# A three-stage decoder kernel: the last bodies of its software pipeline written out by hand for each engine

## The chip, the cores and the metric

The kernel runs on one core of a Trainium2 chip. The metric is device time of one execution in microseconds, the median of several; lower is better. Five engines with instruction streams of their own take part: TensorE (PE, matmuls into the eight banks of PSUM), ScalarE (ACT), VectorE (DVE), GpSimd (POOL) and SyncE (SP, which here issues all DMAs of the steady part). They meet only at semaphores that the kernel counts by hand.

## What is computed

`x` is (16, 256, 512) float32, `ctx` has the same shape.

```
x = layernorm(x + attention(x))           # 16 heads of 32, q/k/v/o with low-rank updates
x = layernorm(x + x * scan(ctx*ctx))      # r = decay*r + ctx^2 along the sequence
h = gelu(silu(bitlinear(x, w1, b1)))      # 512 -> 2048; rms norm, 8-bit rounding of rows, ternary weights
h = layernorm(h) * ln_g + ln_b            # over 2048
x = layernorm(x + bitlinear(h, w2, b2))   # 2048 -> 512
```

## The kernel before, in words

The work is cut into 16 batches of 256 rows, each batch into two tiles (q = 0, 1) of 128 rows. A batch goes through a software pipeline of four steps: body `j` does the attention of batch j, the two first layernorms and the first linear layer (`f`, eight blocks of 512 columns) of batch j-1, the wide layernorm and rounding of batch j-2, and the second linear layer (`y`, 16 matmuls for each tile) and the last layernorm of batch j-3. Each engine has its own `body(j)` with the order of its instructions written out by hand; `alive(j, lag)` leaves out the steps whose batch does not exist. `batches` (L187) runs the body for j = 0 to 18, so that the last three bodies, 16, 17 and 18, only empty the pipeline, in the order that was laid out for a full one.

What the change and the prediction touch:

- TensorE: `qk`, `scores`, `shifted`, `weighted` are attention, in banks 0 to 5. `o` (L1176, L1180, matmuls at L1081), `r` (L1183, matmuls at L1187), `f` (L1190, L1195) and `y` (L1199, L1202) share banks 6 and 7: `take` (L1150) finds the last user of the bank and waits for the instruction that read it. `y` reads `hqT`, of which there is one.
- SyncE: `transpose_z` (L302) moves the rounded tile of h, transposed, into `hqT` by two DMA transposes (L307), after `y` of the tile before it has read `hqT`. `transpose_x` (L294, L299) does the same for the input of `f`. `store_out` (L290) writes a tile of the result.
- ScalarE: `silu` (L615, L621), `gelu` (L624, L627), `h_var` (L630, L637, a square with a sum), `h_norm` (L640, L642), `z_square` (L645, L652), `zq_store` (L609, L612, the rounded tile as bf16, which `transpose_z` reads), `normalise` (L593, L597), `xq_store` (L600, L606).
- VectorE: `layernorm1_sum`, `layernorm2_sum`, `layernorm3_sum` (L846, L854, L940: a sum, then its statistics at L842 and L844), `quantise_x` (L862, from L881 to L901), `z_add` (L904, L907), `z_max` (L909, L912), `quantise_z` (L915: five steps on one column, then the rounding at L937).
- GpSimd: `g_mul` (L476, L479, h times `g_tile`), `neg_mean`, `h_rstd` (L463), `z_rms`, `inverse_std1` to `3` (small steps on one or two columns), `res1`, `res2` (L429, L436), which add bias rows.

The chain of a tile after `gelu` is: `h_var`, `h_rstd`, `h_norm`, `g_mul`, `z_add`, `z_max` and `z_square`, `z_rms`, `quantise_z`, `zq_store`, `transpose_z`, `y`, `layernorm3_sum`, `inverse_std3`, `normalise(3)`, `store_out`. Each engine executes in its own order, so a step that waits holds what stands behind it.

Of the kernel before, what the change touches and what calls it, by code (L numbers as in the profile page):

```python
# [7 lines left out]
F32 = mybir.dt.float32  # L8
# [36 lines left out]
NROWS = 3  # L45
LAST_LAG = 3


def decoder_kernel(nc, x, xT, ctxT, W, L, bq, bk, bv, bo, decay, w1T, b1, ln_g, ln_b, w2T, b2, out):
    b1_scratch = nc.dram_tensor("b1_scratch", (NPART, INNER), BF16, kind="Internal").ap()  # L50

    with ExitStack() as ctx:
# [57 lines left out]
        junk = sb("junk", [P, INNER], BF16)  # L110
        fz = sb("fz", [P, NT, 12], F32)
        fs = sb("fs", [P, NT, 8], F32)

# [32 lines left out]
        u_mul = sem("u_mul")  # L146
        u_tern = sem("u_tern")


# [37 lines left out]
        def batches(body):  # L187

            for j in range(NB + LAST_LAG):
                body(j)  # L190
# [17 lines left out]

        def bank_of(name, index):
            return bank[bank_no[name, index]]  # L210

# [24 lines left out]
        def _(sp):  # L236
# [73 lines left out]
            def body(j):  # L310
                if alive(j, -1):
                    load_xT(j + 1)
                if alive(j, 3):
                    transpose_z(j - 3, 1)
                if alive(j, 3):
                    store_out(j - 3, 0)
                if j == 0:
                    load_ctx(0)
                    load_rows(0)
                    sp.wait_ge(u_b1, 5)  # L320
                    for k in range(NPART):
                        sp.dma_start(b1_scratch[k].rearrange("(p f) -> p f", p=P),
                                     b1_parts[:, k, :]).then_inc(u_b1_out, 16)
                    sp.wait_ge(u_b1_out, 16 * NPART)
                    sp.wait_ge(u_zero, 1)
                    for k in range(NPART):
                        sp.dma_start(b1_rows[k * NPART:(k + 1) * NPART, :], b1_scratch).then_inc(u_b1_in, 16)
                    for n in range(4, 8):
                        ffn_chunk(n)
                else:  # L330
                    if alive(j, 0):
                        load_ctx(j)
                    if alive(j, 3):
                        store_out(j - 3, 1)
                    if alive(j, 1):
                        transpose_x(j - 1)
                    if alive(j, 2):
                        transpose_z(j - 2, 0)
                    if alive(j, 0):
                        load_rows(j)  # L340
            batches(body)
            wait(sp, "out_stored", NB - 1, 32)

# [4 lines left out]
        def _(po):  # L348
# [68 lines left out]
            def inverse_std3(b, q):  # L417

                r = rstd[:, 2, :, q:q + 1]
                wait(po, "ln3", b, 3 * (q + 1))  # L420
                po.tensor_scalar(r[:, R_VE, :], mean_var[:, 2, q, 1:2], 1.0, EPS, ALU.mult,
                                 ALU.add).then_inc(S["rstd3"], 1)
# [53 lines left out]
            def g_mul(b, q):  # L476

                wait(po, "h_normed", b, q + 1)
                po.tensor_tensor(h_of(b, q)[:, :], h_of(b, q)[:, :], g_tile[:, :], ALU.mult).then_inc(S["g_mul"], 1)  # L479

            def z_rms(b, q):
# [6 lines left out]
                wait(po, "z_rms", b, 2 * q + 1)  # L488
                po.tensor_tensor(fz[:, q, Z_RMS:Z_RMS + 1], f[:, H_ZMS:H_ZMS + 1], neg_half[:, 0:1],
                                 ALU.pow).then_inc(S["z_rms"], 1)  # L490
# [11 lines left out]
            def body(j):  # L502
# [35 lines left out]
                if alive(j, 0):  # L538
                    attn_split(j, 3)

            batches(body)


# [3 lines left out]
        def _(ac):  # L547
# [35 lines left out]
            def v_store(b, q):  # L583
                wait(ac, "pv_ready", b - 2, 4)
                wait(ac, "v_ready", b, q + 1)
                ac.activation(v_sb[b % 2][:, q, :], bank_of("v", q), ACT.Identity).then_inc(S["v_stored"], 1)

# [27 lines left out]
            def silu(b, q):  # L615
                for n in range(NF):
                    u = NF * q + n
                    wait(ac, "f_ready", b, u + 1)
                    if n == 0:
                        wait(ac, "hqT_loaded", b - 2, 32 * (q + 1))  # L620
                    ac.activation(h_of(b, q)[:, n * FW:(n + 1) * FW], bank_of("f", u), ACT.Silu,  # L621
                                  scale=qx[:, X_DEQ, q:q + 1]).then_inc(S["silu_done"], 1)
# [63 lines left out]
            def body(j):  # L686
# [76 lines left out]
                if alive(j, 1):  # L763
                    silu(j - 1, 1)
                    gelu(j - 1, 0)
                    gelu(j - 1, 1)

            batches(body)


# [3 lines left out]
        def _(dv):  # L774
# [71 lines left out]
            def layernorm1_sum(b, q):  # L846

                wait(dv, "o_ready", b, q + 1)
                wait(dv, "res1", b, q + 1)
                dv.tensor_tensor(rows_of(b)[:, q, :], bank_of("o", q), rows_of(b)[:, q, :],  # L850
                                 ALU.add).then_inc(S["ln1"], 1)
                statistics(1, b, q, 3 * q + 1, rows_of(b)[:, q, :])

            def layernorm2_sum(b, q):  # L854

                wait(dv, "rT_ready", b, q + 1)
                wait(dv, "norm1", b, q + 1)
                dv.scalar_tensor_tensor(rows_of(b)[:, q, :], bank_of("r", q), SCAN_SCALE, rows_of(b)[:, q, :],  # L858
                                        ALU.add, ALU.mult).then_inc(S["ln2"], 1)
# [44 lines left out]
            def z_add(b, q):  # L904

                wait(dv, "g_mul", b, q + 1)
                dv.tensor_tensor(h_of(b, q)[:, :], h_of(b, q)[:, :], b_tile[:, :], ALU.add).then_inc(S["z_added"], 1)  # L907

            def z_max(b, q):  # L909

                wait(dv, "z_added", b, 2 * q + 1)
                dv.tensor_reduce(fz[:, q, Z_MAX:Z_MAX + 1], h_of(b, q)[:, :], axis=AX_X, op=ALU.max,  # L912
                                 apply_absolute_value=True).then_inc(S["z_added"], 1)

            def quantise_z(b, q):  # L915

                def f(k):
                    return fz[:, q, k:k + 1]

                step = [6 * q]  # L920

                def done(ins):
# [10 lines left out]
                done(dv.tensor_tensor(f(Z_MUL), f(Z_SC), f(Z_RMS), ALU.mult))  # L933
                wait(dv, "ln3", b - 1, 3 * q + 1)
                done(dv.tensor_scalar(f(Z_DEQ), f(Z_INV), w_mean[:, 1:2], None, ALU.mult))
                wait(dv, "z_squared", b, q + 1)
                dv.tensor_scalar(h_of(b, q)[:, :], h_of(b, q)[:, :], f(Z_MUL), ROUND, ALU.mult,  # L937
                                 ALU.add).then_inc(S["z_quant"], 1)

            def layernorm3_sum(b, q):  # L940

                wait(dv, "y_ready", b, q + 1)
                wait(dv, "res2", b, q + 1)
                dv.scalar_tensor_tensor(rows_of(b)[:, q, :], bank_of("y", q), fz[:, q, Z_DEQ:Z_DEQ + 1],
                                        rows_of(b)[:, q, :], ALU.mult, ALU.add).then_inc(S["ln3"], 1)
# [52 lines left out]
            def body(j):  # L998
# [52 lines left out]
                if alive(j, 0):  # L1051
                    scan(j)

            batches(body)


# [3 lines left out]
        def _(pe):  # L1060
# [119 lines left out]
            def o_second_half(j, q):  # L1180
                split_product(bank_of("o", q)[:, :], o_terms(q, (2, 3)), first=False).then_inc(S["o_ready"], 1)

            def r(j, q):  # L1183

                p = take(j, "r", q, "scan_done", j - 1, 5)
                for kc in range(KC):
# [3 lines left out]
            def f(j, u):  # L1190

                q, n = divmod(u, NF)
                p = take(j, "f", u, "xqT_loaded", j - 1, 16)
                for kc in range(KC):
# [157 lines left out]
```

## Time and profile before

| | us |
|---|---|
| median of 3 runs | 1128.77 (1127.43 to 1133.42) |
| the profiled execution, its own time | 1124.67 |
| its span, first to last instruction | 1122.9 |
| busy in the span: PE, DVE, ACT, POOL | 952.4, 887.3, 828.3, 601.0 |
| mean granted clock of TensorE | 0.945 of full speed |

The span is 1.8 us shorter than the profiled execution's time, which is 4.1 us under the median. Times in the rows below are counted from the start of the span. A busy time adds up the instructions of an engine. The record of an instruction also holds the time for which it stood in the engine without being able to run. A timeline row that says x16 is sixteen like instructions in a row, with the time from the first one's start to the last one's end; brackets give the idle time before it and what ended that. The last instruction of body 15 on each engine ends between 998 and 1011 us; what comes after it is bodies 16 to 18.

### The profile page before, as it was taken

The page shows a single profiled execution, that of the slowest core. Times are in us where ns is not written, and L with a number is a line of the kernel's source. Part 1 is how long each engine was busy: PE and PEld are TensorE (multiplying, and loading weights), DVE is VectorE, ACT ScalarE, POOL GpSimd, SP SyncE. Part 2 cuts the span into 40 slices and gives each one's busy share as a digit, 9 for nine tenths or more (in the row PEclk, how much of TensorE's full clock was granted, in tenths as well). Part 3 has the DMA queues.
Part 4 walks back from the last instruction along what each step waited for, and adds up shares of the span by engine and source line. Part 5 has one row for each costly group of instructions (what it writes and reads, how often), then busy time and mean ns, then how long its engine had stood idle before and what let it go on. Part 6 is the DMA issues. An engine that isn't in the chain of part 4 may idle for free.

```text
span 1122.9 us, 23509 instructions
## 1 busy us (share of the span) xinstructions
PE 952.4 (85%) x9388; PEld 653.1 (58%) x9388; DVE 887.3 (79%) x1470; ACT 828.3 (74%) x955; POOL 601.0 (54%) x769
## 2 busy tenths in 40 slices
PE   4878878998989898999999898989899998873424
PEld 2666656675757666665757575766667575531201
DVE  5378858888897979798988989797979898885442
ACT  3456677887879787878788787978787878775651
POOL 3213428384756657482938475565738293747250
PEclk8989898999999999999999999999999999977756
DMA  8512100213131212213221313122221222121112
GB/s 309 208 71 101 43 27 20 69 49 78 49 78 20 75 52 51 62 53 69 48 79 49 78 48 78 20 70 57 50 58 57 69 48 60 49 59 28 40 28 66
DMA packets 106350, 73.67 MB, mean 66 GB/s; under 512 B 91385, under 2 KB 91385, under 8 KB 104450
## 3 DMA queue, kind: packets, MB, share of 16 engines
q1 hardware_dynamic: 105522, 70.34, 23.4%
q8 instruction: 75, 1.23, 0.5%
q10 hardware_dynamic: 720, 1.84, 0.5%
q14 instruction: 33, 0.27, 0.1%
HBM read 41.73 MB, written 8.40 MB: 45 GB/s over the span
## 4 chain that ended last, share of the span: by engine, by line
PE 49%; DVE 31%; ACT 7%; issue 6%; DMA 4%; POOL 2%; SPq 1%; POOLq 0%; ACTq 0%; DVEq 0%
PE bank L1081 17%; PE bank L1202 10%; PE bank L1195 9%; DVE neg_max L793 3%; PE wave L1128 3%; DVE fz L912 3%; DVE h L907 3%; DVE stats L842 3%; PE bank L1140 2%; PE wave L1104 2%; DMA xqT<-xq 2%; PE bank L1144 2%; PE bank L1196 2%; DVE xq L898 2%; DVE rows L858 2%
## 5 line engine op out<-in xcount | busy, mean ns | idle before, releaser
L793 DVE TENSOR_REDUCE neg_max<-wave 128x8 f32<-128x2048 f32 x64 | 146.2, 2285 | 56.8 <-PE wave L1104 56.8
L1195 PE MATMUL bank<-w,xqT 128*128 128x512 fp8e4 x512 | 133.9, 385 | 44.9 <-DMA xqT<-xq 36.9
L479 POOL TENSOR_TENSOR h<-h,g_tile 128x2048 f32<-128x2048 f32 x32 | 148.4, 4638 | 40.4 <-ACT h L642 40.4
L1202 PE MATMUL bank<-w,hqT 128*128 128x512 fp8e4 x512 | 124.7, 400 | 43.3 <-DMA hqT<-h 43.3
L559 ACT ACTIVATE probs<-wave 128x1024 f32<-128x1024 f32 x128 | 124.0, 1021 | 30.9 <-PE wave L1128 30.8
L621 ACT ACTIVATE h<-bank,qx 128x512 f32<-128x512 f32 x128 | 87.0, 687 | 44.6 <-PE bank L1196 44.3
L597 ACT ACTIVATE rows<-rows,rstd 128x512 f32<-128x512 f32 x96 | 74.4, 807 | 55.7 <-POOL rstd L394 19.7
L1202 PEld LDWEIGHTS bank<-w,hqT 128*128 128x128 bf16 x512 | 49.7, 102 | 112.2 <-issue 62.0
L1195 PEld LDWEIGHTS bank<-w,xqT 128*128 128x128 bf16 x512 | 48.5, 99 | 110.6 <-issue 47.1
L378 POOL TENSOR_SCALAR attn_hi<-attn 128x256 fp32r<-128x256 f32 x64 | 26.2, 409 | 157.5 <-DVE attn L826 148.7
L907 DVE TENSOR_TENSOR h<-h,b_tile 128x2048 f32<-128x2048 f32 x32 | 75.5, 2359 | 36.5 <-POOL h L479 36.5
L612 ACT ACTIVATE h<-h,neg_round 128x2048 bf16<-128x2048 f32 x32 | 63.9, 1997 | 32.8 <-DVE h L937 32.8
L1081 PE MATMUL bank<-xT_hi,wq_hi 128*128 128x256 f32 x256 | 78.4, 306 | 8.7 <-DVE wk_lo L787 7.7
L1104 PE MATMUL wave<-qk_parts 32*128 32x256 f32 x1536 | 62.9, 293 | 21.4 <-ACT probs L559 21.3
L433 POOL TENSOR_TENSOR rows<-rows,bo_tile 128x512 f32<-128x512 f32 x32 | 54.7, 1728 | 48.6 <-DMA rows<-x 48.6
L1128 PE MATMUL wave<-qk_parts 32*128 32x256 f32 x1536 | 73.3, 302 | 8.6 <-ACT shift_rows L581 8.6
L652 ACT ACTIVATE junk<-h 128x2048 bf16<-128x2048 f32 x32 | 61.1, 1909 | 24.9 <-DVE h L907 24.8
L381 POOL TENSOR_TENSOR attn_lo<-attn,attn_hi 128x256 fp32r<-128x256 f32 x64 | 73.7, 1152 | 5.3
L642 ACT ACTIVATE h<-h,fs 128x2048 f32<-128x2048 f32 x32 | 66.9, 2090 | 13.1 <-POOL fs L473 13.1
L1128 PEld LDWEIGHTS wave<-qk_parts 32*128 32x128 f32 x1536 | 56.9, 191 | 30.0 <-ACT shift_rows L581 15.4
L1140 PE MATMUL bank<-probs,v_sb 128*32 128x256 f32 x1024 | 69.7, 390 | 4.4 <-ACT probs L559 4.4
L1081 PE MATMUL bank<-xT_lo,wq_hi 128*128 128x256 f32 x256 | 73.3, 286 | 0.0
(151 smaller groups left out, 2821.3 us busy)
## 6 DMA issues: line engine op xcount, KB each, us to landing
ctx_sb<-ctxT SPq DMA_DIRECT2D x16, 512.0 KB, 3.7
rows<-x SPq DMA_DIRECT2D x16, 512.0 KB, 4.0
out<-rows SPq DMA_DIRECT2D x32, 256.0 KB, 2.0
xT_in<-xT SPq DMA_DIRECT2D x15, 512.0 KB, 4.7
h<-w1T SPq DMA_DIRECT2D x4, 1024.0 KB, 5.4
h<-w2T SPq DMA_DIRECT2D x4, 1024.0 KB, 5.6
h<-Wq SPq DMA_DIRECT2D x1, 1024.0 KB, 5.8
h<-Wk SPq DMA_DIRECT2D x1, 1024.0 KB, 9.6
```

Source lines behind the costliest of these rows:

```text
L479: po.tensor_tensor(h_of(b, q)[:, :], h_of(b, q)[:, :], g_tile[:, :], ALU.mult).then_inc(S["g_mul"], 1)
L559: ac.activation(probs[:, kt, :, :], wave[:, :, kt * T:(kt + 1) * T], ACT.Exp, scale=SM_SCALE).then_inc(S["probs_ready"], 1)
L597: ac.activation(rows_of(b)[:, q, :], rows_of(b)[:, q, :], ACT.Identity, scale=r[:, R_USED, :], bias=r[:, R_NB, :]).then_inc(S[f"norm{ln}"], 1)
L621: ac.activation(h_of(b, q)[:, n * FW:(n + 1) * FW], bank_of("f", u), ACT.Silu, scale=qx[:, X_DEQ, q:q + 1]).then_inc(S["silu_done"], 1)
L793: dv.tensor_reduce(neg_max[:, :, :], wave[:, :, :].rearrange("p j (t k) -> p j t k", t=NT), axis=AX_X, op=ALU.max, negate=True).then_inc(S ...
L907: dv.tensor_tensor(h_of(b, q)[:, :], h_of(b, q)[:, :], b_tile[:, :], ALU.add).then_inc(S["z_added"], 1)
L1081: last = pe.matmul(psum, lhsT, rhs, start=(first and i == 0), stop=(final and i == len(pairs) - 1))
L1104: last = pe.matmul(bank[head][:, qt * T:(qt + 1) * T], parts[at, qp, qt * P:(qt + 1) * P], parts[at, kp, :], start=(i == 0), stop=(i == 2))
L1128: last = pe.matmul(bank[head][:, kt * T:(kt + 1) * T], keys, queries, start=(i == 0), stop=(i == 3))
L1140: pe.matmul(bank[4][i * HD:(i + 1) * HD, 0:T], v_sb[b % 2][:, kt, ch:ch + HD], probs[:, kt, i, :], start=(kt == 0), stop=(kt == NT - 1))
L1195: pe.matmul(p[:, :], xqT[:, q, kc, :], w1[:, kc, n * FW:(n + 1) * FW], start=(kc == 0), stop=False)
L1202: last = pe.matmul(p[:, :], hqT[:, k, :], w2[:, k, :], start=(k == 0), stop=(k == FC - 1))
```

## The change

`batches` stops after body 15, and each engine gets a `drain()` of its own that names what is left: the rest of batch 13 (`THIRD`), 14 (`PRIOR`) and 15 (`LAST`). The order in the drains puts the steps of batch 15 ahead of like steps of batch 14 where both are ready.

- Banks: in the drain `o`, `r`, `f` and `y` use all eight (`drain_bank`), each with a wait of its own for the last reader.
- Buffers: the tiles of batch 14 and 15 are transposed into `hqT`, the two halves of `probs` and a `v_sb`, so each `y` has its own. `y` of the three later tiles waits for each half (8 matmuls) by itself.
- `g_mul` of tile 0 of batches 14 and 15 goes from GpSimd to VectorE (`gain`); tile 1 stays.
- In batch 15 the rounding at L937 and the store at L612 are cut into two halves of 1024 columns each.
- `z_square` of batch 14 stands between the two `silu` of batch 15; both `zq_store` of batch 14 stand after `h_norm` of batch 15.
- `fz_last` gives batch 15 its own column values, and some waits are added that go with it.

```diff
+        drain_bank = {("o", LAST, 0): 7, ("o", LAST, 1): 6, ("r", LAST, 0): 2, ("r", LAST, 1): 3,
+                      ("y", THIRD, 0): 0, ("y", THIRD, 1): 1, ("y", PRIOR, 0): 4, ("y", PRIOR, 1): 5,
+                      ("y", LAST, 0): 6, ("y", LAST, 1): 7}
+        drain_bank.update({("f", LAST, u): (4, 5, 6, 7, 0, 1, 2, 3)[u] for u in range(8)})
...
# SyncE
+            def drain_transpose(b, q):
+                for i in range(2):
+                    if b == LAST:
+                        sp.wait_ge(d_zq, 2 * q + i + 1)
+                    else:
+                        wait(sp, "zq_stored", b, q + 1)
...
+                    sp.dma_start_transpose(out=drain_hqT(b, q)[:, 8 * i:8 * (i + 1), :],
+                                           in_=half_rows(b, q)[:, i, :]).then_inc(d_hqT[LAST - b, q, i], 16)
+            def drain():
+                transpose_z(THIRD, 1)
+                transpose_x(LAST)
+                store_out(THIRD, 0)
+                store_out(THIRD, 1)
+                transpose_z(PRIOR, 0)
+                drain_transpose(PRIOR, 1)
+                drain_transpose(LAST, 0)
+                drain_transpose(LAST, 1)
+                store_out(PRIOR, 0)
...
# GpSimd
+            def drain():
+                res1(LAST)
+                neg_mean(PRIOR, 0)
+                neg_mean(PRIOR, 1)
+                inverse_std1(LAST)
+                inverse_std2(LAST)
+                x_rms(LAST)
+                h_rstd(PRIOR, 0)
+                h_rstd(PRIOR, 1)
+                inverse_std3(THIRD, 0)
+                inverse_std3(THIRD, 1)
+                g_mul(PRIOR, 1)
+                res2(LAST)
+                z_rms(PRIOR, 0)
+                z_rms(PRIOR, 1)
+                neg_mean(LAST, 0)
+                neg_mean(LAST, 1)
+                h_rstd(LAST, 0)
+                h_rstd(LAST, 1)
+                g_mul(LAST, 1)
+                z_rms(LAST, 0)
+                z_rms(LAST, 1)
...
# ScalarE
+            def drain_zq_store(q):
+                for i in range(2):
...
+                    ac.activation(half_rows(LAST, q)[:, i, :], h_halves[:, i, :], ACT.Identity,
+                                  bias=neg_round[:, :]).then_inc(d_zq, 1)
+            def drain():
+                zq_store(THIRD, 1)
+                normalise(1, LAST, 0)
+                normalise(1, LAST, 1)
+                h_var(PRIOR, 0)
+                h_var(PRIOR, 1)
+                normalise(2, LAST, 0)
+                normalise(2, LAST, 1)
+                h_norm(PRIOR, 0)
+                xq_store(LAST)
+                h_norm(PRIOR, 1)
+                normalise(3, THIRD, 0)
+                normalise(3, THIRD, 1)
+                silu(LAST, 0)
+                z_square(PRIOR, 0)
+                silu(LAST, 1)
+                z_square(PRIOR, 1)
+                gelu(LAST, 0)
+                gelu(LAST, 1)
+                h_var(LAST, 0)
+                h_var(LAST, 1)
+                h_norm(LAST, 0)
+                h_norm(LAST, 1)
+                zq_store(PRIOR, 0)
+                zq_store(PRIOR, 1)
+                z_square(LAST, 0)
+                z_square(LAST, 1)
+                drain_zq_store(0)
+                drain_zq_store(1)
...
# VectorE
+            def drain():
+                layernorm1_sum(LAST, 0)
+                layernorm1_sum(LAST, 1)
+                layernorm2_sum(LAST, 0)
+                layernorm2_sum(LAST, 1)
+                layernorm3_sum(THIRD, 0)
+                layernorm3_sum(THIRD, 1)
+                quantise_x(LAST)
+                gain(PRIOR, 0)
+                z_add(PRIOR, 0)
+                z_max(PRIOR, 0)
+                z_add(PRIOR, 1)
+                z_max(PRIOR, 1)
+                quantise_z(PRIOR, 0)
+                quantise_z(PRIOR, 1)
+                gain(LAST, 0)
+                z_add(LAST, 0)
+                z_max(LAST, 0)
+                z_add(LAST, 1)
+                quantise_z(LAST, 0)
+                z_max(LAST, 1)
+                quantise_z(LAST, 1)
...
# TensorE
+            def drain():
+                wait(pe, "attn_split", LAST, 8)
+                drain_o(0, "silu_done", PRIOR, 8)
+                drain_o(1, "silu_done", PRIOR, 7)
+                wait(pe, "probs_ready", LAST, 8)
+                wait(pe, "scan_done", LAST, 5)
+                for q in range(NT):
+                    r_product(bank_of("r", q, LAST), q)
+                drain_y(THIRD, 0)
+                drain_y(THIRD, 1)
+                wait(pe, "xqT_loaded", LAST, 16)
+                drain_f(0, "attn_done", LAST, 4)
...
+                drain_f(7, "ln2", LAST, 4)
+                for at, (b, q) in enumerate(((PRIOR, 0), (PRIOR, 1), (LAST, 0), (LAST, 1))):
+                    wait(pe, "silu_done", LAST, at + 1)
+                    drain_y(b, q)
```

After the part shown, GpSimd, ScalarE and VectorE each run the last layernorm of batches 14 and 15, tile by tile, and SyncE stores the four tiles.

## Rows read from the trace of the kernel before

**Rows 1.** windows: busy us of each engine, under full load and at the end
```profile
884.00:1004.00 120.00, 105.56 (x1069) 70.23 (x1068) 103.24 (x175) 94.36 (x109) 70.52 (x93) 0.93 0.22 51
1004.00:1123.00 119.00, 47.74 (x173) 20.96 (x171) 50.36 (x78) 60.74 (x57) 47.08 (x64) 0.69 0.17 38
```

**Rows 2.** timeline of TensorE, end: start us, us, engine, line, [idle before <-releaser]
```profile
1004.79 3.62 PE L1202 MATMUL bank<-w,hqT 128*128 128x512 fp8e4 x16
...
1013.48 0.39 PE L1081 MATMUL bank<-wo_hi,attn_lo 128*128 128x512 f32 x1
1022.73 5.37 PE L1202 MATMUL bank<-w,hqT 128*128 128x512 fp8e4 x16 [8.86 <-DMA hqT<-h]
...
1028.94 0.66 PE L1187 MATMUL bank<-ident,ctx_sb 128*128 128x128 f32 x4 [0.41 <-DVE rows L944]
1050.72 1.86 PE L1195 MATMUL bank<-w,xqT 128*128 128x512 fp8e4 x4 [21.12 <-DMA xqT<-xq]
...
1078.70 6.38 PE L1202 MATMUL bank<-w,hqT 128*128 128x512 fp8e4 x16 [14.31 <-DMA hqT<-h]
...
1110.95 5.63 PE L1202 MATMUL bank<-w,hqT 128*128 128x512 fp8e4 x16 [4.72 <-DMA hqT<-h]
```

**Rows 3.** chain of waits, end: DMA transposes, issue and landing
```profile
1047.18 3.40 DMA xqT<-xq
...
1095.84 1.24 SPq L307
...
1097.12 3.23 DMA hqT<-h
```

**Rows 4.** timeline of ScalarE, end
```profile
1004.99 0.69 ACT L621 ACTIVATE h<-bank,qx 128x512 f32<-128x512 f32 x1 [0.39 <-PE bank L1196]
...
1061.67 1.28 ACT L627 ACT_TABLE_LOAD   x1
...
1066.77 1.99 ACT L637 ACTIVATE junk<-h,fs 128x2048 bf16<-128x2048 f32 x1
...
1080.04 2.09 ACT L642 ACTIVATE h<-h,fs 128x2048 f32<-128x2048 f32 x1 [4.01 <-POOL fs L473]
...
1097.98 2.00 ACT L612 ACTIVATE h<-h,neg_round 128x2048 bf16<-128x2048 f32 x1 [2.16 <-DVE h L937]
...
1119.62 0.81 ACT L597 ACTIVATE rows<-rows,rstd 128x512 f32<-128x512 f32 x1 [9.54 <-POOL rstd L426]
```

**Rows 5.** timeline of VectorE, end
```profile
1041.01 1.22 DVE L881 TENSOR_REDUCE qx<-rows 128x2 f32<-128x1024 f32 x1 [3.75 <-ACT rows L597]
...
1043.86 1.23 DVE L893 TENSOR_SCALAR qx<-qx,w_mean 128x2 f32<-128x2 f32 x1
...
1076.77 2.29 DVE L907 TENSOR_TENSOR h<-h,b_tile 128x2048 f32<-128x2048 f32 x1 [10.65 <-POOL h L479]
...
1093.32 2.28 DVE L912 TENSOR_REDUCE fz<-h 128x1 f32<-128x2048 f32 x1
...
1096.66 1.28 DVE L937 TENSOR_SCALAR h<-h,fz 128x2048 f32<-128x2048 f32 x1
...
1116.62 0.75 DVE L944 SCALAR_TENSOR_TENSOR rows<-bank,fz,rows 128x512 f32<-128x512 f32 x1 [8.65 <-PE bank L1202]
...
1118.13 0.18 DVE L844 BATCH_NORM_AGGREGATE mean_var<-stats 128x2 f32<-128x6 f32 x1
```

**Rows 6.** timeline of GpSimd, end
```profile
1076.82 2.29 POOL L467 TENSOR_SCALAR fs<-fs 128x1 f32<-128x1 f32 x1
...
1082.20 4.52 POOL L479 TENSOR_TENSOR h<-h,g_tile 128x2048 f32<-128x2048 f32 x1 [2.20 <-ACT h L642]
```

**Rows 7.** timeline of GpSimd around 943 us: one addition on GpSimd
```profile
942.89 2.13 POOL L433 TENSOR_TENSOR rows<-rows,bo_tile 128x512 f32<-128x512 f32 x1 [3.01 <-DMA rows<-x]
```

**Rows 8.** timeline of VectorE around 944 us: rounding, then one scan
```profile
942.61 1.29 DVE L937 TENSOR_SCALAR h<-h,fz 128x2048 f32<-128x2048 f32 x1
943.81 1.75 DVE L832 TENSOR_TENSOR_SCAN ctx_sb<-decay_col,ctx_sb 128x256 f32<-128x256 f32 x1
```

More of the change, by code:

```diff
@@ L187, in batches @@
         def batches(body):
-            for j in range(NB + LAST_LAG):
+            for j in range(NB):
                 body(j)
@@ L420, in inverse_std3 @@
                 wait(po, "ln3", b, 3 * (q + 1))
+                if b == LAST:
+                    wait(po, "norm3", PRIOR, q + 1)
                 po.tensor_scalar(r[:, R_VE, :], mean_var[:, 2, q, 1:2], 1.0, EPS, ALU.mult,
@@ L539, in body @@
                     attn_split(j, 3)
+            def drain():
[20 more added lines that the diff above has]
+                z_rms(LAST, 1)
+                for b in (PRIOR, LAST):
+                    for q in range(NT):
+                        inverse_std3(b, q)
             batches(body)
+            drain()
         @block.scalar
@@ L766, in body @@
                     gelu(j - 1, 1)
+            def drain_zq_store(q):
+                h_halves = h_of(LAST, q)[:, :].rearrange("p (i k) -> p i k", i=2)
+                for i in range(2):
+                    if i == 0:
+                        ac.wait_ge(d_round, q + 1)
+                    else:
+                        wait(ac, "z_quant", LAST, 6 * (q + 1))
+                    ac.activation(half_rows(LAST, q)[:, i, :], h_halves[:, i, :], ACT.Identity,
[29 more added lines that the diff above has]
+                drain_zq_store(1)
+                for b in (PRIOR, LAST):
+                    for q in range(NT):
+                        normalise(3, b, q)
             batches(body)
+            drain()
         @block.vector
@@ L1052, in body, with gain @@
                     scan(j)
+            def gain(b, q):
+                wait(dv, "h_normed", b, q + 1)
+                dv.tensor_tensor(h_of(b, q)[:, :], h_of(b, q)[:, :], g_tile[:, :], ALU.mult).then_inc(d_gain_dve, 1)
+            def drain():
[20 more added lines that the diff above has]
+                quantise_z(LAST, 1)
+                for b in (PRIOR, LAST):
+                    for q in range(NT):
+                        layernorm3_sum(b, q)
             batches(body)
+            drain()
         @block.tensor
@@ L1305, in _ @@
             batches(body)
+            drain()
 def kernel(**inputs):
```

105 lines of the change are left out of this document (86 added, 19 removed).

## The prediction

> **What bounds the kernel now.** I read the profile's page first, then stretches. Under full load four engines are busy together: in 120 us TensorE 105.6, VectorE 103.2, ScalarE 94.4, GpSimd 70.5. The last 119 us hold only 47.7, 50.4, 60.7 and 47.1 [rows 1], so there no engine is the bound, but a chain of waits. The change leaves bodies 0 to 15 as they are, so I compare only what follows them.
>
> The timeline of TensorE shows that chain. After `y` of batch 13, tile 0 (1004.79) and the two `o` (last matmul 1013.48), the matmuls come in islands: `y` 13,1 at 1022.73, `f` of batch 15 at 1050.72 after 21.1 us idle, `y` 14,1 at 1078.70 after 14.3, and `y` 15,0 and 15,1, of which the last starts at 1110.95 after 4.7 [rows 2]. The last island waits for the single `hqT`: its transposes start only when the `y` before it has ended.
>
> **The change, part by part.** All times are those of the profiled span; "tile 15,1" is batch 15, tile 1.
>
> *A. From the last `silu` of batch 14 to `f` of batch 15.* That `silu` ends at 1005.7 [rows 4]; `o` waits for it, since both of its banks were read by it. `o` twice takes 5.5 (from the end of `y` at 1008.4 to 1013.9), `r` twice 1.3 (0.66 for one) [rows 2]: 1012.5. `y` 13,0, now behind them, 3.6 at full clock [rows 2]: 1016.2. It used to stand ahead, and `transpose_z` of 13,1 waits for it; the tile itself is stored by 1012.8, since `zq_store` now goes first on ScalarE. A pair of transposes takes 1.28 to the second issue and 3.23 to landing [rows 3], 4.65 with the start of the matmul: 1020.9. `y` 13,1 takes 5.4 to 6.4 after a wait [rows 2]; I take 5.6, the row nearest in idle time: 1026.5. Meanwhile VectorE does both layernorm 1 and 2 sums, and ScalarE both `h_var` of batch 14, all over by 1023, so these cost nothing; without that cover `quantise_x` would wait for them. But `layernorm3_sum` of 13,1 stands ahead of `quantise_x` in VectorE's order: **x of batch 15 waits for `y` of 13**, some 5 us. Sum and statistics 1.7 [rows 5]: 1028.2. `quantise_x` took 6.2, from 1041.01 to the issue of its transpose at 1047.18 [rows 5, 3]; two small steps in it, 1.23 [rows 5] and one like it, stood behind the two additions of `res2`, which now come much later, so 4.4: 1032.6. Transpose 3.4 [rows 3] and the start: 1036.2. It was 1050.7: **14.5 us gained**. Behind the waiting VectorE stand `gain` and `z_add` of batch 14; behind `xq_store` on ScalarE `h_norm` 14,1 (to 1034); neither is needed before 1043.
>
> *B. From `f` to the second `h_norm` of batch 15.* From `f` to the last `silu` it took 10.95 [rows 2, 4]. Two `z_square` of batch 14 now stand in it, nearest row `h_var` with 1.99 each [rows 4]. About 1.6 of these 3.9 is hidden, since with eight banks TensorE runs ahead and the last four `silu` run at 0.69 rather than at the 1.08 of a block. So 13.3: 1049.5. Table load 1.28, two `gelu` 3.8, two `h_var` 4.0, two `h_norm` of 2.09 [rows 4]: 1062.7, where the second ended at 1082.1 before: **19.4 in all**. The 4.9 beyond A, in spite of the `z_square`, come from two things that no longer stand before `h_norm` 15,1: 4.0 of waiting [rows 4] for a GpSimd step that was held 2.29 [rows 6] behind a `g_mul`, and a `zq_store`.
>
> *C. From `h_norm` to the last `y`.* `gain` 15,0 on VectorE, 2.29 as `z_add` is (both read two tiles of SBUF) [rows 5], ends at 1063.0. `g_mul` 15,1 is ready at 1062.8 and takes 4.5 [rows 6]; `z_add` 15,0 is ready at 1063.1. Can they overlap? In the rows an addition on GpSimd ready at 942.89 during a rounding lasted until 945.02, though a scan on VectorE was ready at 943.81; the scan ended at 945.56 [rows 7, 8]. The two took turns, and the one that waited came first. So I take GpSimd first: `g_mul` to 1067.6, `z_add` 15,0 to 1069.9, `z_max` 2.2 to 1072.1, `z_add` 15,1 to 1074.4. Then five small steps 1.06 (from 1095.60 to 1096.66) and two half roundings, 0.65 each [rows 5]: 1076.7; `z_max` 15,1 1079.0; small steps and halves 1081.4. ScalarE is then only busy with halves, an estimated 1.1 each from 2.00 for a whole [rows 4]: the last ends at 1082.8. The halves are issued 1.28 apart on SyncE, the last at 1083.1, landed at 1086.3 [rows 3]; the first half of `y` runs under that, its second takes 1.9: **1088.4, where it was 1116.6**, 28.2 in all. The two `zq_store`, four transposes and two `y` of batch 14 (1069 to 1079) stand beside this chain and cost nothing; were they later than 1081, they would delay `y` 15,0.
>
> *D. The last layernorm and store* stay: 6.3 from the end of `y` to the end of the span [rows 2, 5]; ScalarE's last step stands in that [rows 4]. The sums of the three tiles before are over by 1087. Semaphores and waits that are only added are below what a row shows, 0 to 0.5 in all; I take 0.
>
> Sum: span 1094.7, the profiled execution 1124.67 - 28.2 = 1096.5. The median stands 4.1 above the profiled execution; with the same distance the median is 1100.6, say 1100.5.
>
> Two rules against the trace. The Trainium skill (SBUF — State Buffer, "Who interferes with whom") says that a VectorE instruction with two SBUF inputs and a GpSimd instruction that reads SBUF exclude each other, the later one blocking in full. By that rule the new `gain` speaks against the change, and the rows agree with the blocking. Without any block the sum in C would be 3.2 lower.
>
> The Trainium skill (ScalarE: Activation LUTs, "What ACT_TABLE_LOAD costs") gives about 2.66 us for each change of table set, drain included. Here two `gelu` fill the time right behind a load of 1.28 [rows 4], so the trace shows no drain; three more changes would be 8.0 by the page.
>
> **The rivals.**
> - *VectorE keeps its turn, or nothing blocks.* Then `z_add` 15,0 runs at 1063. 2 to 3 us less: 1097.5 to 1098.5. Against it: rows 7 and 8. Chance 0.13.
> - *Reloaded tables.* `z_square` between two `silu` is new; no row shows a square under the table of `silu`. If it needs another table, there are three more loads of 1.28, 3.8 us, all in B: 1104.5. For it: `silu` and `gelu` each have their load. Against it: small functions run under any table seen. Chance 0.14. The Trainium skill (the page on ScalarE, "Table sets: the hidden batching unit") names cheap functions that every set holds, and the square isn't among those it lists.
> - *A slow TensorE.* Its rows of 5.4 to 6.4 come after idle time, 3.6 without [rows 2]. If every `y` of batches 14 and 15 takes 6.4, the last ends 6.3 later: 1107. Against it: `y` 14,0 to 15,0 lie close together. Chance 0.08.
> - *The change does not do what it says*: the last four `y` stay one behind another, each with its transposes, 10.3 apiece from 1069. Then span 1117, time 1122.7, a gain of 6. The waits in the diff don't ask for it. Chance 0.03; half of it within 0.5% of now.
> - *Slower.* GpSimd's small steps, each held up to 2.1 us by a two-input step of VectorE (2.29 at L467 [rows 6]). VectorE has two such steps more. It decides from the point where 16 held steps lie on the chain: 16 x 2.1 = 34, more than the 28.2 gained and the 5.6 that 0.5% is. I count 7 on it in C and D (`z_rms` 2 and 2, the last `inverse_std3` 3), most of them with VectorE idle. Time 1135. Chance 0.02.
>
> **How the numbers follow.** My forecast has 0.58, and another 0.02 is for a gain lost for a reason that I don't see. 0.5% of the time (5.6 us) is about what a measurement of this kernel can tell from no change. All cases but the last ones are faster by more than that: 0.96; same 0.02; slower 0.02. The range takes in the blocking rival with 3 us for the spread of the median (low 1095), the tables and a slow TensorE (1107, and 1 more): 1108.
>
> **What would show it.** In the profile after: `f` of batch 15 near 1036 behind `y` 13,1; `quantise_x` waiting for L944; a `z_add` 15,0 of some 6.7 us in its record, its `g_mul` with 4.8; the two last halves' transposes 1.3 apart; the last `y` ending near 1088. I would be wrong in A if `f` starts before 1032, in B if there are loads around L652, in C if the stretch from `h_norm` 15,1 to the end of `y` is not 24 to 28 us.

## The result and the profile after

| | before | after |
|---|---|---|
| median (4 runs each), us | 1128.83 (1127.43 to 1133.42) | 1099.96 (1096.24 to 1100.72) |
| ratio, 95% interval | | 0.9747 (0.9718 to 0.9776) |
| profiled execution, its time and its span | 1124.67, 1122.9 | 1099.86, 1098.0 |
| mean granted clock of TensorE | 0.945 | 0.962 |

The forecast was 1100.5, range 1095 to 1108. To compare the ends alone I count from the end of the last `silu` of batch 14, the last step of TensorE and ScalarE that both kernels make at the same place, to the end of the span: I call that **the end**. It was 1122.9 - 1005.7 = 117.2 us [rows 4]; after the change it is 1098.0 - 1008.1 = 89.9, so 27.3 less, against 28.2 forecast. Bodies 0 to 15, which are the same in both, took 2.4 us longer in the profiled execution of the changed kernel. The numbers of an end come from one profiled execution of each kernel, those of a median from all executions, and the two need not agree to better than a few us.

The windows of the kernel after, the same two stretches as in [rows 1] (us busy of PE, PEld, DVE, ACT, POOL, then the clock, DMA share, GB/s):

```profile
884.00:1004.00 120.00, 105.42 (x1068) 70.16 (x1068) 103.19 (x173) 94.55 (x108) 71.05 (x93) 0.94 0.22 53
...
1004.00:1098.00 94.00, 46.50 (x183) 21.17 (x182) 64.37 (x86) 62.46 (x61) 40.10 (x62) 0.78 0.21 51
```

Full load is the same. The end now takes 94 us instead of 119. VectorE has 14 us more in it: two `gain` of 2.3 and two `z_add` whose records are each 4.2 longer (below) make 13.

TensorE's timeline after, from the last `silu` on, to hold against [rows 2]:

```profile
1013.82 1.03 PE L1363 MATMUL wave<-ident,ctx_sb 128*128 128x128 f32 x8
1014.69 3.62 PE L1404 MATMUL wave<-w,hqT 128*128 128x512 fp8e4 x16
1022.90 6.36 PE L1404 MATMUL wave<-w,hqT 128*128 128x512 fp8e4 x16 [4.60 <-DMA hqT<-h]
1038.69 1.89 PE L1373 MATMUL bank<-w,xqT 128*128 128x512 fp8e4 x4 [9.42 <-DMA xqT<-xq]
...
1071.89 5.76 PE L1404 MATMUL bank<-w,hqT 128*128 128x512 fp8e4 x16 [22.71 <-DMA hqT<-h]
1077.48 3.62 PE L1404 MATMUL bank<-w,probs 128*128 128x512 fp8e4 x16
1083.45 3.61 PE L1404 MATMUL bank<-w,probs 128*128 128x512 fp8e4 x16 [2.35 <-DMA probs<-h]
1088.06 3.61 PE L1404 MATMUL bank<-w,v_sb 128*128 128x512 fp8e4 x16 [0.99 <-DMA v_sb<-h]
```

The names on the right tell the buffers: `hqT`, then `probs` twice, then `v_sb`. The last `y` waits 0.99 instead of the 4.7 of before, and the four lie within 20 us. Two long waits are left, 9.4 for the transposed x and 22.7 for the tile 14,0; I read the second as free, since batch 15's chain runs beside it.

VectorE's timeline after shows both places where it is on the chain:

```profile
1022.87 0.18 DVE L973 BATCH_NORM_AGGREGATE mean_var<-stats 128x2 f32<-128x6 f32 x1
1029.30 0.75 DVE L1086 SCALAR_TENSOR_TENSOR rows<-wave,fz,rows 128x512 f32<-128x512 f32 x1 [6.25 <-PE wave L1404]
...
1030.92 1.22 DVE L1010 TENSOR_REDUCE qx<-rows 128x2 f32<-128x1024 f32 x1
...
1063.18 2.29 DVE L1199 TENSOR_TENSOR h<-h,g_tile 128x2048 f32<-128x2048 f32 x1 [6.98 <-ACT h L726]
1065.51 6.49 DVE L1041 TENSOR_TENSOR h<-h,b_tile 128x2048 f32<-128x2048 f32 x1
1072.03 2.29 DVE L1046 TENSOR_REDUCE fz_last<-h 128x1 f32<-128x2048 f32 x1
1074.23 2.28 DVE L1041 TENSOR_TENSOR h<-h,b_tile 128x2048 f32<-128x2048 f32 x1
```

L1086 is `layernorm3_sum` 13,1: VectorE is idle 6.25 us for it, and `quantise_x` (L1010) stands right behind. L1199 is `gain` 15,0. L1041 is `z_add`: 6.49 for tile 0, where it had been 2.29 [rows 5], and 2.28 for tile 1. In GpSimd's timeline after stands what it waited for, `g_mul` 15,1:

```profile
1065.21 4.63 POOL L536 TENSOR_TENSOR h<-h,g_tile 128x2048 f32<-128x2048 f32 x1 [2.87 <-ACT h L726]
```

### The profile page after: what moved, and what is told of

It is laid out like the page before. It is cut to its first block, busy times and chain, and to the rows that moved or that the text cites. A ratio compares the mean times of both kernels' runs of the same rounds, so it can differ in the third digit from the quotient of the medians.

```text
span 1098.0 us, 23490 instructions
## 1 busy us (share of the span) xinstructions
PE 954.8 (87%) x9372; PEld 656.1 (60%) x9388; DVE 896.8 (82%) x1474; ACT 828.9 (75%) x957; POOL 591.3 (54%) x767
## 3 DMA queue, kind: packets, MB, share of 16 engines
q8 instruction: 75, 1.23, 0.5%
## 4 chain that ended last, share of the span: by engine, by line
PE 50%; DVE 31%; ACT 7%; issue 6%; DMA 4%; POOL 2%; SPq 0%; another core or an unknown queue 0%; POOLq 0%; ACTq 0%; DVEq 0%
PE bank L1255 18%; PE bank L1373 9%; PE bank L1380 8%; DVE neg_max L922 3%; PE wave L1302 3%; DVE h L1041 3%; DVE stats L971 3%; DVE fz L1046 3%; PE bank L1314 3%; PE wave L1278 2%; DMA xqT<-xq 2%; PE bank L1318 2%; DVE xq L1027 2%; PE bank L1374 2%; DVE qx L1010 2%
## 5 line engine op out<-in xcount | busy, mean ns | idle before, releaser
L536 POOL TENSOR_TENSOR h<-h,g_tile 128x2048 f32<-128x2048 f32 x30 | 139.9, 4664 | 39.1 <-ACT h L726 39.1
L1373 PE MATMUL bank<-w,xqT 128*128 128x512 fp8e4 x496 | 130.4, 386 | 33.9 <-DMA xqT<-xq 25.5
L705 ACT ACTIVATE h<-bank,qx 128x512 f32<-128x512 f32 x124 | 84.2, 687 | 44.3 <-PE bank L1374 41.8
L1373 PEld LDWEIGHTS bank<-w,xqT 128*128 128x128 bf16 x496 | 47.0, 99 | 96.9 <-issue 25.7
L1041 DVE TENSOR_TENSOR h<-h,b_tile 128x2048 f32<-128x2048 f32 x32 | 84.0, 2624 | 18.5 <-POOL h L536 18.5
L1380 PE MATMUL bank<-w,hqT 128*128 128x512 fp8e4 x416 | 94.3, 380 | 0.0
L696 ACT ACTIVATE h<-h,neg_round 128x2048 bf16<-128x2048 f32 x30 | 59.8, 1997 | 27.2 <-DVE h L1073 27.2
L658 ACT ACTIVATE qk_parts<-bank,bias_qk 128x256 fp32r<-128x256 f32 x128 | 53.6, 474 | 28.3 <-PE bank L1255 28.2
L736 ACT ACTIVATE junk<-h 128x2048 bf16<-128x2048 f32 x32 | 61.1, 1909 | 18.2 <-DVE h L1041 18.2
L961 DVE TENSOR_TENSOR_SCAN ctx_sb<-decay_col,ctx_sb 128x256 f32<-128x256 f32 x64 | 73.6, 1208 | 0.0
```

Of the source, the lines that this page charges most:

```text
L1373: pe.matmul(p[:, :], xqT[:, q, kc, :], w1[:, kc, n * FW:(n + 1) * FW], start=(kc == 0), stop=False)
```

## The experiments

Each is the changed kernel with one edit, if nothing else is said. The table gives the profiled execution of each, by the end and by its two parts: from the last `silu` of batch 14 to the first matmul of `f` of batch 15, and from there to the end of the span.

| | to `f` | from `f` | the end | against after | `y` 13,1 took |
|---|---|---|---|---|---|
| before | 45.0 | 72.2 | 117.2 | +27.3 | 5.4 |
| after | 30.6 | 59.3 | 89.9 | | 6.4 |
| e1 one after another | 29.5 | 72.9 | 102.4 | +12.5 | 5.3 |
| e2 gains on GpSimd | 33.7 | 63.9 | 97.6 | +7.7 | 5.3 |
| e3 whole tiles | 30.4 | 60.5 | 90.9 | +1.0 | 6.2 |
| e4 order alone | 34.5 | 75.8 | 110.3 | +20.4 | 6.2 |
| e5 x before `y` 13,1 | 25.1 | 60.8 | 85.9 | -4.0 | 6.0 |
| e6 warm TensorE | 27.8 | 59.1 | 86.9 | -3.0 | 3.6 |
| e7 both gains of 15 on VectorE | 29.3 | 57.9 | 87.2 | -2.7 | 5.2 |
| e8 fused norm | 30.5 | 53.8 | 84.3 | -5.6 | 6.3 |
| e9 = e5 and e8 | 25.1 | 55.1 | 80.2 | -9.7 | 5.1 |
| e10 = e9, warm TensorE | 25.1 | 55.5 | 80.6 | -9.3 | 6.3 |
| e11 two banks ahead | 30.7 | 60.7 | 91.4 | +1.5 | 6.5 |
| e12 gain of 14 on GpSimd | 34.6 | 60.5 | 95.1 | +5.2 | 6.2 |

The last column shows how far two of these ends can be compared. After the change `y` 13,1 starts 14.7 to 14.8 us after that `silu`, behind 4.6 us of idle time, in every run but e6 (which fills that time), and then takes 5.1 to 6.5 us. Where x waits for it, that goes into "to `f`": e1, e3, e7, e8 and e11 have the changed kernel's code up to there and show 29.3 to 30.7 against its 30.6. The first blocks of `f` differ in the same way: from `f` to the second `h_norm` of batch 15 the same code took 26.2 us in e6, 26.5 after the change and 27.7 in e12. So a difference of about 1 us between two ends can be TensorE's, and the changed kernel's own `y` 13,1 was one of the slow ones.

**e1, one tile after another.** In `drain_transpose`, on SyncE:

```diff
+                    wait(sp, "y_ready", b - 1 + q, 2 - q)
                     sp.dma_start_transpose(out=drain_hqT(b, q)[:, 8 * i:8 * (i + 1), :],
```

> Each transpose of the tiles 14,1, 15,0 and 15,1 waits, beside its own tile, until y of the tile before it has ended, as with one hqT; everything else as in the changed kernel. Measure: the end, from the end of the last silu of batch 14 to the end of the span (117.2 us before the change, 89.9 after). Theory (the tiles' own buffers and the unchained y are the largest part of the gain): y 14,0 still starts 63.8 after that silu, and the three others follow it one after another, each 4.65 of transposes and some 5.6 of slow matmuls later, so the last y ends 100.4 instead of 83.6 after the silu; the end is 106 to 107.5 us. Rival (the new order of batches 14 and 15 is what gained, the buffers hardly matter because the chain on VectorE is the bound): the end is under 93.

Measured: 102.4, less than expected but far from the rival. The chain of waits of this run shows the pattern of before again, issue behind `y` and landing ahead of the next:

```profile
1078.56 3.25 DMA probs<-h
...
1081.94 6.26 PE bank L1405 x16
...
1088.28 3.27 DMA probs<-h
...
1091.69 6.51 PE bank L1405 x16
...
1098.27 3.23 DMA v_sb<-h
...
1101.63 4.96 PE bank L1405 x16
```

From one `y` to the next it is 3.4 us, not 4.65: with a semaphore for each half, `y` starts when the first half lands, and the second lands under it. So a part of what I would have put down to the buffers belongs to the wait by halves. The buffers are worth 12.5 us by the end, 13.6 counted from `f`. About half of that is TensorE's: behind waits of 3.5 us the last three `y` took 6.3, 6.5 and 5.0 instead of 3.6 each.

**e2 and e12, the gain back on GpSimd.** In e2 `g_mul` of tile 0 stands ahead of that of tile 1 in GpSimd's drain and `gain` is gone, for both batches; in e12 for batch 14 alone:

```diff
-                gain(PRIOR, 0)
...
+                g_mul(PRIOR, 0)
                 g_mul(PRIOR, 1)
```

> The gain of tile 0 of batches 14 and 15 is back on GpSimd, where both are multiplied one after the other. Theory (GpSimd and VectorE take turns at two-input steps, so that z_add 15,0 waits for the other tile's g_mul in any case): the last z_add ends 0.4 us later if VectorE gets its turn between the two g_mul, 2.6 later if not; the end is 90.3 to 92.5 us, and z_add 15,0 takes its turn after one or both g_mul. Rival (the move of the gain to VectorE is a large part of what was gained, as 4.5 us of GpSimd become 2.3 of VectorE beside it): the end is 94 us or more.

> Only the gain of tile 14,0 is back on GpSimd; that of 15,0 stays on VectorE. In e2 a step of two columns in quantise_x of batch 15 stood 4.37 us behind g_mul 14,0. Theory (that step alone moved f by 3.1 us, the rest of e2's 7.7 came from batch 15's own gain): f starts 33.5 to 34.5 us after the last silu of batch 14, the rest follows as in the changed kernel, and the end is 92.8 to 94 us. Rival (all of e2's loss comes from batch 15): the end is 89.5 to 90.5.

Measured: e2 97.6, in the rival's range, and e12 95.1, later than the 92.8 to 94 expected. For e2 I had seen only batch 15's chain. VectorE's and GpSimd's timelines of e12 show what I had left out:

```profile
1030.61 0.16 DVE L1014 TENSOR_TENSOR qx<-qx 128x2 f32<-128x2 f32 x1
1030.81 4.37 DVE L1015 TENSOR_SCALAR qx<-qx 128x2 f32<-128x2 f32 x1
```

```profile
1030.65 4.49 POOL L536 TENSOR_TENSOR h<-h,g_tile 128x2048 f32<-128x2048 f32 x1
```

A step of two columns in `quantise_x`, normally 0.17, takes 4.37 because `g_mul` 14,0 began 0.16 before it. The same step took 4.37 in e2 and e4, which have the same edit. It is on the way to `f`, which starts 4.0 us later. So the largest effect of the moved gain is on batch 14, which is itself off the chain: the move **clears GpSimd while x is quantised**. The other 1.2 us of e12 are not the edit's: its first blocks of `f` were slow, and the second and third `silu` waited 1.45 and 1.18 for them, where they waited 1.01 and 0.39 after the change.

```profile
1047.65 0.69 ACT L706 ACTIVATE h<-bank,qx 128x512 f32<-128x512 f32 x1 [1.18 <-PE bank L1374]
```

Batch 15's own gain shows in e2 from the second `h_norm` on. From there to the end of the last rounding it is 2.4 us more than after the change, as expected of two `g_mul` in a row: the record of `z_add` 15,0 is 6.57 behind 8.99 of GpSimd. Another 1.3 came because `y` 15,0, behind a longer wait, took 6.08 instead of 3.61. That the two ends differ by only 2.5 is chance: in e2 `y` 13,1 was 0.9 faster than in e12 and the stretch behind it 0.3.

```profile
1067.95 8.99 POOL L536 TENSOR_TENSOR h<-h,g_tile 128x2048 f32<-128x2048 f32 x2 [0.88 <-ACT h L728]
```

```profile
1090.52 6.08 PE L1404 MATMUL bank<-w,probs 128*128 128x512 fp8e4 x16 [4.28 <-DMA probs<-h]
```

**e3, whole tiles.** One rounding and one store of 2048 columns for each tile of batch 15 (`if b <= LAST` ahead of the whole rounding; one activation that counts both halves).

> Rounding and store of batch 15 are done by whole tiles again; the two transposes of a tile follow its whole store. Theory: the last store ends 0.3 later than its second half does now, the first transpose is issued only then and the second 1.3 later, so the last y ends 1.0 us later and the end is 90.8 us (90.4 to 91.3). Rival (the halves save the half of rounding, store and matmuls, 3 us or more): 92.9 or more.

Measured: 90.9, as expected, so the halves are worth about 1.0 us, which is no more than the ends can tell. They hide little, I take it because the two transposes are issued one behind the other in any case.

**e11, two banks ahead.**

```diff
                 wait(pe, reader, b, count_read)
+                if u >= 2:
+                    wait(pe, "silu_done", LAST, u - 1)
                 f_product(bank_of("f", u, LAST), u)
```

> Each block of f of batch 15 from the third on also waits for the silu of the block two before it, as with two banks. Theory: blocks 5 and 6 are there when z_square 14,0 ends, 7 and 8 are each 0.4 to 0.5 late, so the banks are worth 0.8 to 1.1 us here: the end is 90.7 to 91.0 us. Rival (with TensorE held, the clock falls and y or f slow down): 92 or more.

Measured: 91.4, 1.5 later and a little above the range expected. ScalarE's timeline shows the mechanism: the last two `silu` wait, 0.84 and 0.39, where all four ran together (2.53 for four) after the change.

```profile
1048.47 1.25 ACT L705 ACTIVATE h<-wave,qx 128x512 f32<-128x512 f32 x2
1050.56 0.69 ACT L705 ACTIVATE h<-wave,qx 128x512 f32<-128x512 f32 x1 [0.84 <-PE wave L1374]
1051.64 0.69 ACT L705 ACTIVATE h<-wave,qx 128x512 f32<-128x512 f32 x1 [0.39 <-PE wave L1374]
```

**e4, the order alone.** e1, e2, e3 and e11 together.

> All four together: y one after another, the gains on GpSimd, whole tiles, and f of batch 15 limited to two banks' worth of blocks ahead of silu (0.8 to 1.1 by itself). What is left of the change is the order alone. Theory: the end is 107.5 to 111 us, so that the order alone gives 6 to 10 of the 27.3 us and the buffers 16 or more; the time is 0.7% below the kernel before. Rival (order is nearly all): the end is under 97.

Measured: a median of 1115.34 us, ratio to before 0.9895 (0.9865 to 0.9924), the end 110.3. By the ends the order gives 6.9 of the 27.3 us. By the medians it is 12 (1127.65 - 1115.34; the interval allows 9 to 15), and only one execution of the kernel before was profiled, so how much the order gives is not settled between 7 and 15 us. The edit also leaves in two things that aren't order: the banks of `o`, `r` and `y`, and `y`'s wait by halves.

What the profiled execution shows is where the order gains and where it loses. The second `h_norm` of batch 15 ends 63.5 us after the last `silu`, where it was 76.4 before, in spite of e2's step in `quantise_x`. But `y` 14,0 starts at 70.0 instead of 55.1, and the four `y` then stand one behind another for 34.0 us. This order needs the buffers.

**e5, x before `y` 13,1.**

```diff
-                layernorm3_sum(THIRD, 1)
                 quantise_x(LAST)
+                layernorm3_sum(THIRD, 1)
```

> On VectorE layernorm3_sum of tile 13,1 stands behind quantise_x instead of ahead of it. Theory (x of batch 15 waits for y of 13, and for nothing else): quantise_x starts right after the second layernorm's normalise, 5.5 us earlier than now; f starts 5 to 5.5 us earlier, and as everything up to the last y hangs on it, the end is 84.4 to 85.2 us. Rival (ScalarE or GpSimd takes its place at once: h_norm and g_mul of batch 14, whose steps now meet the chain of batch 15): the end is 88 or more.

Measured: `f` starts 5.5 earlier, as expected, but 1.5 of it is lost behind it: the end is 85.9. Most of that, 1.1, is lost on ScalarE, whose timeline shows a new wait:

```profile
1033.59 0.80 ACT L681 ACTIVATE rows<-rows,rstd 128x512 f32<-128x512 f32 x1
1038.78 0.81 ACT L681 ACTIVATE rows<-rows,rstd 128x512 f32<-128x512 f32 x1 [4.39 <-POOL rstd L482]
1039.61 1.28 ACT L705 ACT_TABLE_LOAD   x1
1040.90 2.42 ACT L705 ACTIVATE h<-bank,qx 128x512 f32<-128x512 f32 x4
```

`normalise(3)` of 13,1 stands ahead of the first `silu` and waits 4.39 for its deviation, since `layernorm3_sum` 13,1 was moved back; the first four `silu` then run together, behind blocks of `f` of which the first two had long been there. The rest is at `y` 15,0. The window there shows a granted clock of 0.69 where the changed kernel has 1.00, and it takes 5.16 instead of 3.61, after nearly the same idle time (2.33 and 2.35). "To `f`" was 25.1 in e5, in e9 and in e10, to 0.01 us, while `y` 13,1 took 6.0, 5.1 and 6.3 in them: x no longer waits for `y` of 13.

```profile
1081.00:1086.20 5.20, 5.13 (x17) 2.07 (x18) 3.84 (x8) 3.00 (x3) 1.97 (x6) 0.69 0.63 121
```

The changed kernel's `y` 15,0:

```profile
1083.40:1087.10 3.70, 3.61 (x16) 1.49 (x16) 3.60 (x7) 2.24 (x3) 1.00 (x3) 1.00 0.48 92
```

**e6, a warm TensorE.**

```diff
                 drain_y(THIRD, 0)
+                for _ in range(22):
+                    pe.matmul(bank[5][:, :], b1_rows[:, 0:P], w2[:, 0, :], start=True, stop=True)
                 drain_y(THIRD, 1)
```

> 22 matmuls of 128x512 into an unused bank stand between y 13,0 and y 13,1 (they add no output). Theory: TensorE keeps its full clock over the 4.6 us of idle time, y 13,1 takes 3.6 instead of 6.4, and 2.7 us arrive at the end: 87.2 us (86.8 to 88.2; if the 22 reach past the landing they cost up to 0.5). Rival (y is slow after a wait for another reason, such as its first use of new data): y 13,1 stays at 5.4 or more, the end at 89.5 or more.

Measured: `y` 13,1 takes 3.62 instead of 6.36, and all of the 2.7 arrives: 86.9. Against another execution it could have been less, as the same `y` took 5.1 to 6.5 in the other runs; the gain is 1.5 to 2.9 us. The windows are after's `y` 13,1 and then e6's, with the granted clock behind POOL:

```profile
1022.90:1029.20 6.30, 6.30 (x16) 2.17 (x16) 0.15 (x1) 3.77 (x5) 4.94 (x17) 0.56 0.00 0
```

```profile
1026.60:1030.20 3.60, 3.60 (x17) 1.46 (x16) 0.16 (x1) 1.68 (x4) 2.99 (x11) 1.00 0.00 0
```

A mean of 0.56 is nearly all at the 1.2 GHz level, after 4.6 us of idle time; 1.00 is 2.4 GHz, with TensorE busy to the last moment.

**e7, both gains of batch 15 on VectorE**, in the order gain, `z_add`, gain, `z_add`, `z_max`, with semaphores of their own for `z_add` and `z_max`.

> In batch 15 the gain of tile 1 is on VectorE too, in the order gain, z_add, gain, z_add, z_max, and no g_mul is left beside it. Theory (z_add 15,0 stands 4.2 us in its record because g_mul 15,1 has the turn): each of the four steps takes 2.3, the second z_add ends 9.2 after the first h_norm instead of 13.4, and the last rounding, which VectorE's own work then sets, 2.2 to 2.5 earlier; the end is 87.4 to 88 us. Rival (z_add is slow for another reason, such as both engines on the same tiles of SBUF): z_add stays above 4 us, and the end is 92 or more.

Measured: none of the four steps is held, and the end is 87.2. VectorE's timeline of e7:

```profile
1065.85 2.29 DVE L1210 TENSOR_TENSOR h<-h,g_tile 128x2048 f32<-128x2048 f32 x1 [8.04 <-ACT h L727]
1068.18 2.29 DVE L1045 TENSOR_TENSOR h<-h,b_tile 128x2048 f32<-128x2048 f32 x1
1070.39 2.29 DVE L1210 TENSOR_TENSOR h<-h,g_tile 128x2048 f32<-128x2048 f32 x1
1072.71 2.29 DVE L1045 TENSOR_TENSOR h<-h,b_tile 128x2048 f32<-128x2048 f32 x1
```

From the start of `gain` 15,0 to the end of the last rounding it is 18.5 us instead of 21.0. This 2.5 is the edit's. The 2.7 of the ends holds two differences more, both TensorE's, that nearly cancel: `y` 13,1 was 1.2 faster, the stretch from `f` to the second `h_norm` 1.1 slower. So GpSimd is no help with this step here: its 4.5 us hold VectorE, which does the same in 2.3. The Trainium skill (SBUF — State Buffer, "Who interferes with whom") says that the two engines share one pair of SBUF ports as an exclusive lock, and that a VectorE instruction with two SBUF inputs contends for it with a GpSimd instruction that reads SBUF. Both traces agree: `z_add` 15,0 took 6.49 with `g_mul` beside it and 2.29 without.

**e8, the fused norm.** `h_norm`, `g_mul` and `z_add` of batch 15 become

```diff
+                    dv.scalar_tensor_tensor(h_of(b, q)[:, :], h_of(b, q)[:, :], fs[:, q, H_NMEAN:H_NMEAN + 1],
+                                            g_tile[:, :], ALU.add, ALU.mult)
...
+                    dv.scalar_tensor_tensor(h_of(b, q)[:, :], h_of(b, q)[:, :], fs[:, q, H_RSTD:H_RSTD + 1],
+                                            b_tile[:, :], ALU.mult, ALU.add)
```

> Batch 15's wide layernorm is two steps on VectorE: (h + negative mean) * g, then that * rstd + b; h_norm of ScalarE and g_mul of GpSimd are gone for this batch. Theory: the first step starts at the end of h_var 15,0 rather than of h_norm 15,0, 4.1 us earlier; with e7's saving the last rounding ends 6.4 us earlier and the end is 83.0 to 84.5 us, if the two-operand step with a column takes 2.3 like the plain one. Rival (such a step takes longer, or batch 14's zq_store and y, which it catches up with, become the wait): 86 or more.

Measured: 84.3. A step takes 2.35 to 2.38.

**e9 and e10, put together.**

> The two changes together that gained: quantise_x ahead of layernorm3_sum 13,1, and batch 15's wide layernorm as two steps on VectorE. Theory (each takes time out of a different stretch of the same chain): f starts 25.1 us after the last silu of batch 14, and from there the stretch is that of the fused kernel, so the end is 79 to 81 us and the time 10 below the changed kernel, 1089 to 1091 with the spread of the first 15 bodies. Rival (batch 14's y, which can't start before its zq_store, become the wait): the end is 83 or more.

> e9 with matmuls that add no output: 19 between y 13,1 and f, and 10 between y 14,1 and y 15,0, into banks that nobody reads then. Theory (the halved clock after idle time costs where TensorE is on the chain, at the first blocks of f and at y 15,0): f's four first silu are over 1.8 us earlier, y 15,0 takes 3.6, and the end is 1.5 to 2.5 us below e9's. Rival (the fillers run into the landing of x and push f, or TensorE's clock is off the chain): the end is within 0.5 us of e9's or above it.

Measured: e9 has a median of 1090.57 us (1088.89 to 1091.32), ratio to before 0.9667 (0.9644 to 0.9691). It adds the two gains in full (4.0 + 5.6 against 9.7), and no run is clearly below it. e10 has 1089.98, ratio 0.9674 (0.9648 to 0.9701), and an end of 80.6: not faster than e9, the rival's case. With e5's edit in it, the first `silu` again waits for `normalise(3)` of 13,1 (4.38 in e10) and not for TensorE, so a faster `f` has nobody to serve; and `y` 15,0, which the second filler was for, took 3.61 in e9 without it. To move `normalise(3)` behind `silu` too was not tried.

## Why the prediction was right

The mechanism came as forecast, stretch by stretch. That the median comes within 0.6 us of the forecast 1100.5 is partly luck. The forecast for the profiled execution was 1096.5, and it was 1099.86: 2.4 of the difference is in bodies 0 to 15, 0.9 in the end. The forecast then added 4.1, the distance from the profiled execution to the median before; after the change that distance was 0.1.

**A, to `f`: forecast 14.5 earlier, it was 45.0 - 30.6 = 14.4.** The wait of x for `y` of 13 is shown by e5. That `y` is slow after a wait because of TensorE's clock is shown by e6; 5.6 was taken for it and 6.36 measured, 0.8 too little, which the shorter way to its start (14.8 after the last `silu`, forecast 15.2) and small terms behind it made up for; the two steps of `res2` in `quantise_x` went as forecast (L1022 took 0.22 instead of 1.23, so the stretch 4.35). What the text had not said is that this last gain, and the normal length of the other small steps, hang on the moved `gain` of 14,0. I costed the move of the gains in part C alone, and the 4.2 us by which e12's step is held are in none of its sentences: the sum came out right since the order in the diff was followed, not because the step was understood.

**B, to the second `h_norm`: forecast 57.0 after the last `silu`, it was 57.0** (from 1008.1 to 1065.1). No load stands around the two `z_square` (L736) between the `silu` (L705), so that rival is gone: a square runs under the table of `silu`.

```profile
1045.48 1.90 ACT L736 ACTIVATE junk<-h 128x2048 bf16<-128x2048 f32 x1
...
1047.38 2.53 ACT L705 ACTIVATE h<-wave,qx 128x512 f32<-128x512 f32 x4
1049.80 1.90 ACT L736 ACTIVATE junk<-h 128x2048 bf16<-128x2048 f32 x1
...
1051.81 1.28 ACT L711 ACT_TABLE_LOAD   x1
```

The estimate of 1.6 us hidden by the banks agrees with e11's 1.5. Of the 4.9 that B gains beyond A the prediction names two sources, 4.0 of waiting and a `zq_store`. They make about 6 against 2.3 of `z_square`, so 3.7; the missing 1.2 is the wait ahead of `h_norm` 15,0 in the kernel before, which is gone too:

```profile
1070.05 2.09 ACT L642 ACTIVATE h<-h,fs 128x2048 f32<-128x2048 f32 x1 [1.20 <-POOL fs L473]
```

**C, to the last `y`: forecast 25.7, it was 26.5** (1065.1 to 1091.7). The turn of GpSimd came as in [rows 7, 8], `z_add` 15,0 took 6.49 where 6.7 was forecast. Up to the end of the last rounding it is 0.3 over. One term there is mis-sized: the five small steps waited 0.5 us for `z_rms` on GpSimd, whose own step was held 2.53 by `z_add` 15,1 (L1041):

```profile
1074.39 2.53 POOL L546 TENSOR_TENSOR fz_last<-fs,neg_half 128x1 f32<-128x1 f32 x1
```

Being a single step, it is all that came, on the chain, of the rival on the slower side. The other 0.5 is behind the last rounding, 7.5 us to the end of `y` where 7.0 was forecast. The sum added 1.9, the second eight matmuls of `y`, to the landing of the last half. But the first eight had not ended by then. All sixteen run from the landing of the first half on, which takes 3.75 (1087.92 to 1091.67). In the chain of waits:

```profile
1084.68 3.24 DMA v_sb<-h
...
1088.06 3.63 PE bank L1404 x16
```

The rival without any block is refuted by the 6.49. The prediction puts it 3.2 us lower and shows no working; by its own times the last `z_add` would end 4.5 earlier. e7, where nothing blocks but VectorE also does the fourth large step, is 2.5 lower.

**D** stayed at 6.3. The sum was thus 28.2 against 27.3 in the ends. The medians are 28.9 apart.

What the large parts are, by taking them out one at a time: own buffers 12.5 (e1), the two gains off GpSimd 7.7 (e2, of which TensorE's clock is about 1), banks 1.5 (e11), halves 1.0 (e3), and 6.9 for the order, measured alone (e4; 12 by the medians). They add up to 29.6 against 27.3 by the ends. Each has an uncertainty of 1 us or more, that of the order of several, so no overlap can be read from this sum.

## What to carry to other kernels

At the end of a software pipeline look for what was left of the full one: a single buffer that makes tiles follow each other, and an order that puts a batch with time to spare ahead of the last one. When two engines hold each other, as VectorE and GpSimd do here, price a move by what it does to every step of the other engine that falls beside it, small ones on the chain above all; here that was worth 4.2 us, the step itself 2.4. And ask whether the slower engine should take part at all: two steps on VectorE alone beat three engines in turn by 5.6 us (e8). And before comparing single executions, look for a stretch with the same code in both and see how far it differs.

## What the runs showed of the hardware

- A step of 128x2 on VectorE is held as long as a large one: 4.37 us instead of 0.17 beside a `g_mul` of 4.49 (e12). GpSimd's column steps are held as well (2.53 instead of 0.55).
- TensorE's clock fell in a wait of 4.6 us (0.56 in `y` 13,1), and after 2.3 us of idle time it was full in the changed kernel and 0.69 in e5. The length of the wait alone doesn't decide it: `y` 15,0 took 3.61, full speed, behind 2.98 (e11) and 3.84 us (e3), but 5.16 behind 2.33 (e5), 6.08 behind 4.28 (e2) and 6.5 behind 3.50 (e1). Behind the same 4.6 us, `y` 13,1 took 5.1 to 6.5 in twelve executions. So the same wait can cost 1.5 us or nothing, and a single execution doesn't settle a difference of that size.
- Bodies 0 to 15, with the same order and operations in every kernel here, ended (last `silu` of batch 14) between 1003.3 and 1012.6 us after the start of the span in the fourteen profiled executions. I did not look for the cause. Counting from that point leaves TensorE's 1 to 1.5 us as the difference between single executions of the same code.
